# A DLRM tower on one core: which of two engines copies which T pair out of PSUM

## What is computed

```python
e = jnp.stack([tbl_f[ids[:, f]] for f in range(32)], axis=1)      # 512 x 32 x 64
h, outs = e, []
for i, (W, b) in enumerate(((W0, b0), (W1, b1), (W2, b2))):       # 128 rows of weights each
    Wr = W.reshape(128, h.shape[1], 32)
    nxt = jnp.einsum('bjk,bzk,ojz->bok', h, e, Wr) + b[None, :, None]
    if i != 2:
        h, o = nxt[:, :64], nxt[:, 64:]
    else:
        o = nxt
    outs.append(o)
z = jnp.sum(jnp.concatenate(outs, axis=1), axis=2)
y = relu(relu(concat([z, dense_ctx]) @ W_top1 + b_top1) @ W_top2 + b_top2) @ W_top3
```

## Time and profile before

| what | value |
|---|---|
| median of 3 runs | 660.75 us (659.64 to 661.15) |
| profiled execution, its time | 659.79 us |
| profiled execution, its span | 658.1 us |
| TensorE busy | 626.3 us, 95% of the span |
| VectorE busy | 483.4 us, 73% |
| ScalarE busy | 214.7 us, 33% |
| GpSimd busy | 128.6 us, 20% |
| mean granted TensorE clock | 0.982 of full speed |

### The profile page before, as it was taken

The page is one execution under the profiler, slowest core; times in us unless marked ns, Lnnn a source line. Parts: engine busy times, 40 slices in busy tenths (PEclk is TensorE's granted clock), DMA queues, the critical chain, the costliest instruction groups (busy, mean ns, idle before and its releaser), DMA issues.

```text
span 658.1 us, 32257 instructions
## 1 busy us (share of the span) xinstructions
PE 626.3 (95%) x14488; PEld 520.0 (79%) x14488; DVE 483.4 (73%) x497; ACT 214.7 (33%) x354; POOL 128.6 (20%) x137
## 2 busy tenths in 40 slices
PE   6844999999999999999999999999999999999998
PEld 6843778888888888888888888888888888888773
DVE  4538778888888888888888888888888888841000
ACT  2421444334433444323233323233333333332012
POOL 7765234444445444000000000000000000000000
PEclk9886999999999999999999999999999999999999
DMA  5110011111111111000000000000000000011000
GB/s 182 30 29 19 20 27 26 28 29 28 27 21 27 30 28 26 13 13 13 12 12 12 12 12 12 12 12 12 12 12 12 12 12 12 12 29 54 11 1 0
DMA packets 31658, 14.87 MB, mean 23 GB/s; under 512 B 24177, under 2 KB 28897, under 8 KB 31378
## 3 DMA queue, kind: packets, MB, share of 16 engines
q1 hardware_dynamic: 27442, 10.26, 7.3%
q0 software_dynamic: 4192, 4.25, 2.9%
HBM read 8.03 MB, written 0.00 MB: 12 GB/s over the span
## 4 chain that ended last, share of the span: by engine, by line
PE 90%; POOL 5%; issue 2%; DVE 1%; DMA 1%; ACT 0%; POOLq 0%; DVEq 0%; ACTq 0%
PE psT L440 20%; PE psX L383 20%; PE psT L464 8%; PE psT L450 7%; PE psT L424 7%; PE psT L427 6%; POOL G_sb L249 5%; PE psX L427 5%; PE psX L424 4%; PE psX L394 3%; PE psX L511 2%; PE psX L403 1%; PE psT L525 1%; PE psX L541 1%; PE psX L283 1%
## 5 line engine op out<-in xcount | busy, mean ns | idle before, releaser
L440 PE MATMUL psT<-T_sb,W1d 64*64 64x256 f32 x1024 | 234.3, 379 | 0.0
L444 PE MATMUL psT<-T_sb,W1d 64*64 64x256 f32 x1024 | 234.3, 379 | 0.0
L450 PE MATMUL psT<-T_sb,W1d 64*64 64x256 f32 (+3 forms) x2048 | 205.3, 300 | 0.0
L730 DVE TENSOR_TENSOR prod<-X 128x1024 f32 (+3 forms) x208 | 171.2, 891 | 17.3 <-PE psT L427 17.1
L767 DVE STREAM_TRANSPOSE PT<-prod 128x4608 f32<-128x4608 f32 x31 | 154.0, 4968 | 0.0
L440 PEld LDWEIGHTS psT<-T_sb,W1d 64*64 64x64 f32 x1024 | 131.3, 133 | 27.8 <-issue 14.4
L464 PE MATMUL psT<-T_sb,W1d 64*64 64x64 f32 (+2 forms) x1536 | 141.7, 270 | 0.0
L444 PEld LDWEIGHTS psT<-T_sb,W1d 64*64 64x64 f32 x1024 | 131.3, 133 | 0.0
L383 PE MATMUL psX<-PT,W0T 32*64 32x256 f32 x4464 | 128.5, 377 | 2.7 <-issue 2.5
L383 PEld LDWEIGHTS psX<-PT,W0T 32*64 32x64 f32 x4464 | 113.8, 131 | 20.5 <-issue 19.0
L450 PEld LDWEIGHTS psT<-T_sb,W1d 64*64 64x64 f32 x2048 | 123.6, 133 | 0.8
(11 more groups left out here) (86 smaller groups left out, 559.2 us busy)
## 6 DMA issues: line engine op xcount, KB each, us to landing
X<-T_sb SPq DMA_DIRECT2D x64, 64.0 KB, 2.0
kept<-grams SPq DMA_DIRECT2D x128, 16.5 KB
G_sb<-in_L_rec_W SPq DMA_DIRECT2D x2, 1024.0 KB, 6.6
E_q<-in_tbl,ids_g POOLq DMA_INDIRECT x96
prod<-in_W_top SPq DMA_DIRECT2D x2, 512.0 KB, 3.5
G_sb<-in_L_rec_W SPq DMA_DIRECT2D x1, 512.0 KB, 5.7
G_sb<-in_tbl,ids POOLq DMA_INDIRECT x32, 2.4
dT<-dT SPq DMA_DIRECT2D x3, 32.0 KB, 3.1
```

Source lines behind the costliest of these rows:

```text
L440: mm(psT[low, 0, 0:HF * SMP], W1d[low, HF + k, :], cross.rearrange("p v (z y) s -> p v z y s", y=HF)[:, :, :, k, :], start=start, stop=sto ...
L444: mm(psT[high, 0, 0:HF * SMP], W1d[low, k, :], T_flat[low, SMP * row:SMP * (row + HF)], start=start, stop=stop, tile_position=(0, C))
L450: last = mm(out[:, SMP * 4 * a:], W1d[high, HF * v + k, :], T_flat[high, SMP * (row + 4 * a):SMP * (row + HF)], start=start, stop=stop and ...
L730: return tt(out, x[:, :, z0:z0 + nz].unsqueeze(3).broadcast_to(shape), x[:, :, y0:y0 + ny].unsqueeze(2).broadcast_to(shape), ALU.mult)
```

## The change

The tuples change places in pairs 0 to 5: ScalarE now copies pairs 1, 3 and 5, whose banks are in `psX`, besides 6 and 7; VectorE copies 0, 2 and 4, in `psT`. Five and three copies stay five and three. The waits of TensorE follow: for pairs 4, 6 and 7 it waits for VectorE, for pair 5 and for H it waits for ScalarE. Step 0's eight copies are still all ScalarE's.

```diff
-T_BY_ACT, T_BY_DVE = (0, 2, 4, 6, 7), (1, 3, 5)
+T_BY_ACT, T_BY_DVE = (1, 3, 5, 6, 7), (0, 2, 4)
@@ in t_matmuls(n, e)
-                    if t == 4:
+                    if t in (4, 6, 7):
+                        pe.wait_ge(t_by_dve, ND * n + {4: 1, 6: 2, 7: 3}[t])
+                    if t == 5:
                         pe.wait_ge(t_by_act, NA * n + 1)
-                    if t == 5:
-                        pe.wait_ge(t_by_dve, ND * n + 1)
-                    if t in (6, 7):
-                        pe.wait_ge(t_by_act, NA * n + t - 4)
@@ in step(n, lookups), ahead of h_matmuls(n + 1)
-                pe.wait_ge(t_by_dve, ND * (n + 1))
+                pe.wait_ge(t_by_act, NA * n + 3)
@@ after the loops
-            pe.wait_ge(t_by_dve, ND * STEPS)
+            pe.wait_ge(t_by_act, NA * STEPS - 2)
```

## The result

The changed kernel takes 663.1 us in the median of 7 runs (660.95 to 664.78), beside 659.64 us for the kernel before in 7 runs (657.46 to 661.15). The ratio is 1.0055, with a 95% interval of 1.0039 to 1.0071: slower by 3.5 us by the medians and 3.6 by the ratio. A second set of runs later gave 1.0044 (1.0027 to 1.0062). The forecast median, 664.5 us, was built on the 660.75 us of the first three runs of the kernel before; its seven runs have 659.64, which is most of the distance to 663.1.

The account below looks back on a forecast made before the run. TensorE, busy 95% of the span, was taken as the bound, with no slack at pair 7's wait on pair 4. Adding 31 x 0.12 = 3.7 us to 659.79 gave 663.5, expected median 664.5 us, range 660.9 to 668.5.

Parts of the forecast that it names:

- Pair 4's slower copy, 0.12 us a step, nothing covers it: In T, VectorE's copy of pair 4 takes 825 ns, not 707, so pair 7 starts 0.12 us later each step.
- Pairs 0, 1 and 2 cost nothing: In T, their swapped copies ahead of pairs 4, 5 and 6 cost 0; the slow stream covers pair 0's lateness.
- pair 4 holding back the slow stream: Rival in T: pair 4's late start delays L427 too; 0.39 us a step, 12.1 us, 672.9 us; chance 4%.
- a rule of strict order: Trainium skill's rule that TensorE matmuls start and end strictly in program order; by it the sum would be 672.9 us.
- VectorE's queue: Rival: addition and copies of pairs 0, 2, 4 lack slack; up to 14.9 us, 7.8 allowed in range; chance 15%, small instruction included.
- Pair 5 to ScalarE gives nothing: Ahead of H, pair 5's copy ends 0.12 us earlier, gain 0: TensorE's stream bounds even steps, T's end odd ones.
- the sign that the prediction named: In the changed profile, H should start 0.12 us later in both even and odd steps.
- The extra instruction before G2 is free: One more small TensorE instruction ahead of G2 was taken as 0, with 6.5 us over 31 steps as upper bound.
- The sum: 31 steps x 0.12 = 3.7 us on the profiled 659.79 us gives 663.5; expected median 664.5 us, 0.56% slower.
- the main term: Pair 4's copy by VectorE delays pair 7 by 0.12 us a step, 31 x 0.12 = 3.7 us.
- The rival of no change: H's gate in even steps is pair 5's copy: even steps gain 0.09, odd pay 0.12; 0.6 us, 661.3; chance 13%.
- the faster one: Rival: H follows pair 5's copy alone in both parities, gaining 0.12 us a step, 3.7 us, to 657.0; chance 8%.

Follow-up runs that it names:

- a dose of 0.32: Kernel before with VectorE copying pairs 1, 3 and 4, ScalarE 0, 2, 5, 6, 7; pair 7 starts 0.32 us later; ratio 1.0143.
- the known gate: Kernel before with H made to wait for ScalarE's copy of pair 6 as well; ratio 1.0171 (1.0149 to 1.0193).
- the run with the extra instruction: Kernel before with a needless wait added ahead of G2 in TensorE's queue, copies unchanged; ratio 1.0011 (1.0000 to 1.0022).
- the kernel without the extra instruction: Changed kernel, but pair 5's copy raises its own semaphore by 3, so the added small instruction ahead of G2 is gone; ratio to kernel before 1.0041.
- the written-out loops: Kernel before with TensorE's loops written out for two steps an iteration, without the If/Else and its jump; copies as before; ratio 1.0095.
- the half copy: Two-steps-an-iteration loops, with pair 4's copy shared by bank: VectorE 0, 2, half of 4; ScalarE 1, 3, other half, 5, 6, 7; ratio to kernel before 1.0363.

## Why the prediction was right, point by point

- **Pair 4's slower copy, 0.12 us a step, nothing covers it.** Right and shown for the start of pair 7 and for even steps. Pair 7 moved by 0.12 in even steps; moving pair 4 without pair 0 brought the whole cost (1.0046); a dose of 0.32 brought 0.27 to 0.32.
- **Pairs 0, 1 and 2 cost nothing.** Right; pair 0 is shown alone (0.9991). VectorE's copy began even 0.09 us before the recorded end of its addition, so the cover was a little thicker than I took it for. Of the rivals, pair 4 holding back the slow stream is refuted by the same run. The prediction tied this rival to a rule of strict order, and that doesn't follow: by its own numbers pair 4's two streams would both start at 513.84, and order kept costs nothing. VectorE's queue had slack: it stood idle for 0.25 us before its copy of pair 4.
- **Pair 5 to ScalarE gives nothing.** This step was wrong for odd steps. I read them as bound by the end of T. They stood at the gate of pair 5's copy, 0.24 us behind it, which the known gate measured as 0.23 to 0.24. The prediction compared the parities and took the larger delay, of the even steps, as proof that neither was at the gate; it only shows that the even ones weren't. T would have let H start about 0.04 us sooner, and the earlier copy gives that back: pair 7 to H shrinks from 0.75 to 0.72 in the changed kernel, and steps whose pair 7 is 0.12 to 0.13 later than in the run with the extra instruction grow by 0.08 and 0.10 in odd steps, 0.12 in even ones. In the kernel without the extra instruction only the odd steps without lookups pay less than 0.12 (0.03 by the medians); in those with lookups pair 7 to H stays at 0.75 though the copy had ended 0.43 us before H, and they pay 0.12. Why is open. For even steps the reading was right: they are bound by TensorE's own stream, as the gate's equal 0.23 and the written-out loops (0.94 down to 0.75) show. So the sign that the prediction named, H 0.12 us later in both parities, came true in one kind of step of four: the changes are 0.13, 0.21, 0.18 and 0.02 us in the order of the table.
- **The extra instruction before G2 is free.** Mis-sized: 0.5 to 0.6 us of the stretch with this division and 0.9 with the old one, of which 0.7 is the first step; in the 27 steps 0.7 to 0.9 and 0.4.
- **The sum.** 3.7 us forecast, 3.6 measured, but as 2.4 to 2.9 for the copies (some or all of the odd steps paid less than 0.12) and 0.4 to 0.9 for the instruction. The mechanism of the main term was right; that the sum came out this close is luck, as two errors cancelled. The rival of no change needed the even steps at pair 5's gate, the faster one needed pair 7's lateness to be absorbed; neither was so.

No version clearly beat the kernel before. Moving pair 0 alone is the nearest, and its interval holds 1.

## What to carry to other kernels

When two engines share the evacuation of banks that are used again within a step, ask of each copy which wait it ends and how much slack that wait has; the faster engine belongs to the copy in front of the wait without slack, here pair 4. Where matmuls run as two streams, measure the slack on the slow one: an idle weight load of 0.2 us in front of the fast one cost nothing. And compare a gate's delay between places that share it before saying what bounds them; two places with different delays can't both be at the gate, but the one with the smaller delay can.

## What the runs showed of the hardware that was not expected

- A needless wait, one more small instruction of TensorE, changed steps by +0.13, +0.06 and -0.08 us, according to their place in the loop, though no data was late.
- Loops of twice the length saved 0.12 us a step and lost it several times over in single standstills of TensorE of 3.4 to 5.1 us; instruction traffic rose from 0.33 to 0.77 MB, and packets of it moved during each of these standstills.
- H followed the last copy that it waited for by 0.23 to 0.24 us, whichever engine made the copy.
- A copy of 128 x 320 fp32 out of one bank took 719 (ScalarE) and 720 ns (VectorE), beside 706 and 825 for 128 x 640 out of two. In the half copy each element stands alone in `T_sb`, 16 elements from the next; in the whole one they stand in pairs. Whether that is the cause wasn't tried.
